# Head projection in rounded parts, and new orders around it, in a two-layer transformer kernel

## The chip, the cores and the metric

The kernel is one program on one core of a Trainium2 chip. The core has TensorE (PE in the profile) for matrix products and transposes into PSUM, VectorE (DVE), ScalarE (ACT) and GpSimd (POOL) for elementwise work, and SyncE (SP), which issues the DMAs. Each engine runs its own queue in order; semaphores tie them together. The metric is the device time of one execution in microseconds.

## The reference

The input x has 8 batches of 512 rows of 128 numbers. Each of two layers adds an attention part and a feed-forward part, both computed from the same normed rows.

Layer 0, attention: 16 heads of 64 (8 pairs), causal softmax, and an output projection of all heads. Layer 0, feed-forward: a shared expert and 32 experts of width 64, of which a router picks six per row with weights. Layer 1, attention: RMS norm, 4 query and 2 key heads of 32, normed queries and keys, output projection. Layer 1, feed-forward: three blocks of linear, layer norm, gelu, linear, with dequantized weights.

```
z   = einsum('dvh,bhcv->bcd', W, y) * (sqrt(d_embed / d_value) / num_heads)   # heads' projection
out = einsum('teh,te->th', y, combine) + shared_out                           # experts
x   = x + attention(xn) + ffn(xn)                                             # each layer
```

## The kernel before, in words

**Layer 0** goes batch by batch. A batch has eight attention rounds, one for each pair of heads, and then 17 units (the shared expert and 16 pairs of experts).

Most products of layer 0 are split products: each operand is kept as a rounded high part (type fp32r) and the rest as a low part, and `split_matmul` issues three products, high by high, high by low, low by high. ScalarE makes the high part with a copy. VectorE or GpSimd subtracts it to make the low part. The transposes, the products with the softmax rows and the heads' projection take plain float32 operands.

On TensorE, `slot` is one round: transposes of the last round's softmax rows (`turn_step`, steps 0, 1, 4, 3, 2), the projection of the next round's queries and keys (`project_qk`), the scores in three chunks (`score0`, `score_rest`) and the last round's values (`weigh_pair`). On ScalarE and VectorE `first_layer` is written in the same order.

`units` follows. For each unit u TensorE projects gate and up (`project_unit`), and three units later multiplies the hidden rows into ACC, a PSUM bank (`unit_down`). Between them ScalarE applies silu, VectorE multiplies by the up part (`gate`) and by the expert weights (`hidden`), ScalarE rounds (`high_part`), and the low part is subtracted by GpSimd for the units in `POOL_LO`, otherwise by VectorE (`low_part`). The rows of the next batch are transposed after unit 5, their router products come after unit 7 (`router_logits`), queries and keys after 9, values after units 12 to 15.

The outputs of the attention pairs, `yt`, are divided by the softmax sums on GpSimd (`divide_pair`), with the reciprocals spread over the partitions by a DMA into one of three `rrow` buffers. The tables `POOL_LO` and `SUMS_AFTER` give the unit after which each pair comes.

The heads' projection (`project_out(b, i)`, two pairs a call) adds `w_out0` times `yt` to ACC. Its four calls stand in `first_head`, at the beginning of the next batch: before and between the last three `unit_down`, and between the first score chunks. After the fourth ScalarE copies ACC.

**Layer 1** goes in two groups of four batches: the linear blocks and the projections of attention first, then eight attention rounds, then the output rows. Its order is written out by hand on each engine. On GpSimd `inv_sqrt`, `inv_norms` and `norm_qk` serve the norms, `add_rows1` adds the residual. The last linear step (`lin_out`, k = 2) adds the hidden rows by a product with the identity. The last batch's four projection calls stand around the first linear steps of layer 1. The last batch's output is one division, one set of products, one addition and one store.

## Time and profile before

| | us |
|---|---|
| median of 3 runs | 1227.32 (1227.23 to 1228.21) |
| the profiled execution | 1227.05 |
| its span in the trace | 1225.3 |
| instructions | 24028 |
| granted TensorE clock, mean | 1.0 of full speed |

The page gives for each engine how long it was busy. TensorE's matmul records overlap, since they are pipelined: a record's length is longer than the distance to the next start, and costs are best read from starts. LDWEIGHTS (PEld) run beside the products. A plain float32 product appears as two records, a rounded one as one. In a timeline row the first number is the start, the second the time from there to the end of the last of the merged instructions, "x4" the number merged.

### The profile page before, as it was taken

The numbers are of one execution on the slowest core, as the hardware profiler recorded it, in microseconds if no ns is written. First come the engines' busy times: TensorE is split into PE (matmuls) and PEld (weight loads), VectorE is DVE, ScalarE is ACT, GpSimd is POOL, SyncE is SP. The second block draws the span as 40 slices with busy tenths as digits, with TensorE's granted clock in tenths as the row PEclk, the third lists the DMA queues.
The fourth block names the chain that finished last, engine by engine and source line by source line (L and its number), as shares of the span: only waits on it lengthen the run. The fifth ranks groups of instructions, "written<-read, shape, count | busy, mean of one in ns | idle before, by whom it ended". The sixth has DMA issues, their size and how long they took to land.

```text
span 1225.3 us, 24028 instructions
## 1 busy us (share of the span) xinstructions
PE 1199.7 (98%) x8956; PEld 893.6 (73%) x8956; DVE 984.0 (80%) x1900; ACT 821.7 (67%) x2174; POOL 409.0 (33%) x362
## 2 busy tenths in 40 slices
PE   8999999999999999999999999999999999999997
PEld 6777677767776777677767786778677777767765
DVE  6878588968896889688968886889687877888786
ACT  6775577557756775677557755775577667777775
POOL 2216410640063007300630073007200859326910
PEclk9999999999999999999999999999999999999999
DMA  7004200410041014100410041004000500000000
GB/s 255 1 29 141 88 1 29 128 55 2 29 135 49 1 30 139 43 2 29 146 37 1 30 147 36 1 29 153 30 1 30 170 13 1 10 10 19 1 10 27
DMA packets 44275, 63.93 MB, mean 52 GB/s; under 512 B 8128, under 2 KB 18368, under 8 KB 43904
## 3 DMA queue, kind: packets, MB, share of 16 engines
q1 hardware_dynamic: 44160, 62.39, 16.1%
q8 instruction: 72, 1.18, 0.4%
q14 instruction: 43, 0.35, 0.1%
HBM read 59.48 MB, written 2.88 MB: 51 GB/s over the span
## 4 chain that ended last, share of the span: by engine, by line
PE 83%; DVE 7%; ACT 4%; POOL 2%; issue 1%; DMA 1%; SPq 1%; DVEq 0%; POOLq 0%
PE psum L1440 14%; PE psum L1396 14%; PE psum L1462 12%; PE psum L64 11%; PE psum L66 10%; PE psum L65 10%; PE psum L1499 4%; PE psum L1405 2%; ACT probs L734 2%; PE psum L1348 1%; DVE mneg L1098 1%; PE psum L1466 1%; DVE sg L1148 1%; DMA crow<-weights 1%; DVE stats L1207 1%
## 5 line engine op out<-in xcount | busy, mean ns | idle before, releaser
L734 ACT ACTIVATE probs<-psum,mneg 128x512 f32<-128x512 f32 (+3 forms) x640 | 329.9, 529 | 132.9 <-DVE mneg L1098 128.6
L1098 DVE TENSOR_REDUCE mneg<-psum 128x2 f32<-128x1024 f32 (+2 forms) x320 | 254.3, 820 | 118.4 <-PE psum L1405 118.2
L1440 PE MATMUL psum<-ident,probs 128*128 128x128 f32 x1600 | 224.8, 278 | 8.9 <-ACT pt L755 3.9
L1089 DVE COPY pt<-psum 128x512 f32<-128x512 f32 x320 | 205.9, 682 | 31.5 <-PE psum L1440 29.1
L1440 PEld LDWEIGHTS psum<-ident,probs 128*128 128x128 f32 x1600 | 176.4, 140 | 42.8 <-issue 24.4
L543 POOL TENSOR_TENSOR qk_lo<-sg,qk_hi 128x512 fp32r<-128x512 f32 x64 | 91.9, 1441 | 167.5 <-ACT qk_hi L778 167.5
L1462 PE MATMUL psum<-pt,v_all 128*64 128x384 f32 (+5 forms) x1088 | 142.6, 412 | 0.0
L507 POOL TENSOR_TENSOR rstd<-var,mhalf 128x4 f32<-128x4 f32 x7 | 7.1, 1011 | 404.5 <-DVE var L987 404.5
L734 ACT ACTIVATION_READ_ACCUMULATOR probs<-psum,mneg 128x1 f32 x640 | 132.3, 207 | 0.0
L1396 PE MATMUL psum<-qk_hi 64*128 64x512 f32 (+7 forms) x640 | 121.5, 375 | 1.3 <-ACT probs L734 1.1
L1462 PEld LDWEIGHTS psum<-pt,v_all 128*64 128x64 f32 (+1 forms) x1088 | 69.5, 135 | 66.2 <-issue 50.7
L64 PE MATMUL psum<-xt_hi,gu_hi 128*128 128x512 f32 x272 | 110.7, 407 | 0.0
L66 PE MATMUL psum<-xt_hi,gu_lo 128*128 128x512 f32 x272 | 107.7, 396 | 0.0
L65 PE MATMUL psum<-xt_lo,gu_hi 128*128 128x512 f32 x272 | 107.5, 395 | 0.0
L539 POOL TENSOR_TENSOR yt<-yt,rrow 128x512 f32<-128x512 f32 x64 | 99.7, 1563 | 23.0 <-DMA rrow<-sums 22.8
L1148 DVE TENSOR_TENSOR sg<-sg,crow 128x512 f32<-128x512 f32 x88 | 97.8, 1111 | 9.3 <-DMA crow<-weights 6.3
L1396 PE MATMUL psum<-qk_lo,qk_hi 64*128 64x512 f32 (+7 forms) x640 | 103.5, 319 | 0.0
L1396 PE MATMUL psum<-qk_hi,qk_lo 64*128 64x512 f32 (+7 forms) x640 | 103.4, 318 | 0.0
L788 ACT ACTIVATE sg<-psum 128x512 f32<-128x512 f32 x96 | 57.1, 595 | 56.3 <-PE psum L66 56.1
L1396 PEld LDWEIGHTS psum<-qk_hi 64*128 64x128 f32 (+1 forms) x640 | 60.1, 184 | 46.4 <-issue 44.3
L1138 DVE TENSOR_TENSOR sg<-sg,psum 128x512 f32<-128x512 f32 x96 | 65.3, 680 | 21.7 <-ACT sg L788 21.7
L778 ACT ACTIVATE qk_hi<-sg 128x512 fp32r<-128x512 f32 x96 | 60.3, 628 | 31.2 <-DVE sg L1148 31.2
(261 smaller groups left out, 2436.2 us busy)
## 6 DMA issues: line engine op xcount, KB each, us to landing
crow<-weights SPq DMA_DIRECT2D x256, 128.0 KB, 3.0
rrow<-sums SPq DMA_DIRECT2D x128, 128.0 KB, 3.0
gu_raw<-in_gu SPq DMA_DIRECT2D x1, 2176.0 KB, 11.4
x_all<-in_x SPq DMA_DIRECT2D x8, 256.0 KB, 6.4
out_rows<-x_all SPq DMA_DIRECT2D x8, 256.0 KB, 2.3
down_raw<-in_down SPq DMA_DIRECT2D x1, 1088.0 KB, 13.5
wqkv_raw<-in_wqkv SPq DMA_DIRECT2D x1, 896.0 KB, 6.7
wqkv_raw<-in_wqkv SPq DMA_DIRECT2D x1, 512.0 KB, 4.9
```

What stands on the lines that cost most here:

```text
L64: nc.tensor.matmul(out, lh, rh, start=start, stop=False, **kw)
L65: nc.tensor.matmul(out, lh, rl, start=False, stop=False, **kw)
L66: return nc.tensor.matmul(out, ll, rh, start=False, stop=stop, **kw)
L539: pool.tensor_tensor(yt[:, p, :], yt[:, p, :], rrow[:, n % RROWS, :], ALU.mult).then_inc(y_divided, 1)
L543: pool.tensor_tensor(hm_lo[u % 3], sg[u % 3], hm_hi[u % 3].bitcast(F32), ALU.subtract).then_inc(pool_lo_ready, 1)
L734: last = act.activation(probs[:, h * HALF + PROB[t]:h * HALF + PROB[t] + w], bank[score_bank(rnd, c) + h][:, o:o + w], ACT.Exp, bias=mneg[ ...
L1089: dve.tensor_copy(turned_rows(rnd)[:, s % 2, :, 3 - s // 2, :], bank[TURN_BANK[s]].rearrange("p (j q) -> p j q", q=P)).then_inc(pt_ready, 1)
L1098: last = dve.tensor_reduce(mneg_h[:, :, t], psum[:, b:b + 2, o:o + P * (t + 1)], AX, ALU.max, negate=True)
L1148: dve.tensor_tensor(sg[u % 3], sg[u % 3], crow[:, m % CROWS, :], ALU.mult).then_inc(hm_ready, 1)
L1396: mm(bank[score_bank(rnd, c) + h][:, o:o + w], ql[r, 0, qs_], kl[r, 1, ks], start=i == 0 and n == 0, stop=False, **K)
L1440: last = nc.tensor.transpose(bank[TURN_BANK[s]][:, i * P:(i + 1) * P], probs[:, v:v + P], ident[:, :])
L1462: last = mm(Y[c:c + m, first * P:T], v(k), rows_t[:, k, first:TILES, :].rearrange("p t q -> p (t q)"), start=(k == 0), stop=(k == TILES - ...
```

## The change

It has these parts.

- **Heads' projection in rounded parts.** The weights are split once in batch 0 (ScalarE rounds, GpSimd subtracts). For each batch ScalarE rounds the eight divided pairs (`high_values`, after the units in `Y_HIGH_AFTER`). GpSimd subtracts pairs 0 to 3 (after the divisions of pairs 4, 5 and 6), VectorE pairs 4 to 7 (after units 14 and 15 and behind the last unit). `project_out` issues split products.
- **Batch ends.** The third call of `project_out` moves behind the second score chunk. For the last batch all four calls stand behind its last `unit_down` and between the first transposes of layer 1.
- **Slots.** In rounds 2 to 6 the projection of the next queries moves from before the first score chunk to behind step 4, next to that of the keys. ScalarE takes the queries behind its copy of step 4. VectorE's router work stands before the second row maximum.
- **Router.** High and low weights lie side by side: the rows' high part is multiplied by all 64 columns at once, the low part by the 32 high ones. VectorE adds the two halves.
- **Layer 1.** The identity product of `lin_out` becomes a transpose that accumulates. GpSimd's `add_rows1` come earlier. The last batch's values, division, output rows, addition and store go in two halves of 256 rows. The table load after the last softmax is gone.
- **Space.** `stats`, `ss1`, `rn1`, the third `rrow` and `acc_cols` share room with other tensors.

```diff
+        Y_HIGH_AFTER = {8: [0], 11: [1, 2], 12: [3], 13: [4], 14: [5], 15: [6], 16: [7]}
+        POOL_Y_LO = {4: [0], 5: [1, 2], 6: [3]}
+        VECTOR_Y_LO = {14: [4], 15: [5], 16: [6, 7]}
+        LAST_POOL_Y_LO, LAST_VECTOR_Y_LO = [[0, 1], [4]], [[2, 3], [5, 6, 7]]
...
+            def low_values(b, pairs):                     # GpSimd; VectorE has the same with y_lo_ready
+                for p in pairs:
+                    pool.wait_ge(y_hi_ready, b * PAIRS + p + 1)
+                    pool.tensor_tensor(y_lo[:, p, :], yt[:, p, :], y_hi[:, PAIRS - 1 - p, :].bitcast(F32), ALU.subtract).then_inc(pool_y_lo_ready, 1)
             def units(b):
                 for u in POOL_LO:
                     low_part(b, u)
                     for p in POOL_LO[u]:
                         divide_pair(b, p)
+                        if b < B - 1:
+                            low_values(b, POOL_Y_LO.get(p, []))
...
-                inv_sqrt(0, 2)
-                add_rows1(1)
...
+                    for g in range(3):                    # first group; the second has them between inv_sqrt(0, g)
+                        add_rows1(g)
...
+            def high_values(b, pairs):
+                for p in pairs:
+                    act.wait_ge(y_divided, b * PAIRS + p + 1)
+                    act.activation(y_hi[:, PAIRS - 1 - p, :], yt[:, p, :], ACT.Copy).then_inc(y_hi_ready, 1)
...
+                    if b < B - 1 or u < UNITS - 2:
+                        high_values(b, Y_HIGH_AFTER.get(u, []))
...
-                chain.step(dve.tensor_reduce(sm, lg, AX, ALU.max, negate=True))
+                chain.step(dve.tensor_copy(rl[:, :, :], lg[:, :, 1, :]))
+                chain.step(dve.tensor_tensor(rl[:, :, :], rl[:, :, :], lg[:, :, 0, :], ALU.add))
+                chain.step(dve.tensor_reduce(sm, rl[:, :, :], AX, ALU.max, negate=True))
...
+                        if u < UNITS - 1:
+                            low_values(b, VECTOR_Y_LO.get(u, []))
                 low_part(b * UNITS + UNITS - 1, UNITS - 1)
+                if b < B - 1:
+                    low_values(b, VECTOR_Y_LO[UNITS - 1])
...
                 for p in (2 * i, 2 * i + 1):
-                    last = mm(ACC, w_out0[:, p, :], yt[:, p, :], start=False, stop=(p == PAIRS - 1), **K)
+                    last = split_matmul(nc, ACC, (w_out_hi[:, p, :], w_out_lo[:, p, :]), (y_hi[:, PAIRS - 1 - p, :], y_lo[:, p, :]), False, p == PAIRS - 1, **K)
...
-                    last = split_matmul(nc, logits_bank(b)[:, t * E:(t + 1) * E], (xt_hi[:, b % 2, c], xt_lo[:, b % 2, c]), (rw_hi[:, :], rw_lo[:, :]), True, True)
+                    mm(logits_bank(b)[:, o:o + 2 * E], xt_hi[:, b % 2, c], rw[:, :], start=True, stop=False, **K)
+                    last = mm(logits_bank(b)[:, o:o + E], xt_lo[:, b % 2, c], rw_hi, start=False, stop=True, **K)
...
-                if p < PAIRS - 1:
-                    pe.wait_ge(y_ready, n - 1) if p > 1 else pe.wait_ge(qk_lo_ready, n * 2 + 1)
+                if p == 1:
                     project_qk(n + 1, [0])
...
+                elif p < PAIRS - 1:
+                    pe.wait_ge(y_ready, n - 1)
+                    project_qk(n + 1, range(2))
...
                 first_chunks(b)
+                score0(b * PAIRS, 1)
                 if b:
                     project_out(b - 1, 2)
-                score0(b * PAIRS, 1)
...
-            project_out(B - 1, 0)
             unit_down(B - 1, UNITS - 3)
...
+            unit_down(B - 1, UNITS - 1)
+            project_out(B - 1, 0)
             lin_in(0, 0, 2)
...
-                        mm(bank[g][:, c], ht[g][:, c], ident[:, :], start=False, stop=False, **K)
+                        mm(bank[g][:, c], ht[g][:, c], ident[:, :], is_transpose=True, start=False, stop=False, **K)
...
+                def last_rows(g):
+                    for half in range(2):
+                        pe.wait_ge(y_divided, ROUNDS0 + n0 + g + 1 + half)
+                        for t in range(2 * half, 2 * half + 2):
+                            c = slice(t * P, (t + 1) * P)
+                            last = mm(last_banks(half)[1][:, c], y1t[g][:, c], wo1[:, :], start=True, stop=True)
+                        last.then_inc(rows_done, 1)
```

## Rows read from the trace of the kernel before

**Rows 1.** The page, busy time of each engine and its share of the span.
```profile
PE 1199.7 (98%) x8956; PEld 893.6 (73%) x8956; DVE 984.0 (80%) x1900; ACT 821.7 (67%) x2174; POOL 409.0 (33%) x362
```
**Rows 2.** The page, chain that ended last, by engine.
```profile
PE 83%; DVE 7%; ACT 4%; POOL 2%; issue 1%; DMA 1%; SPq 1%; DVEq 0%; POOLq 0%
```
**Rows 3.** Busy time by stretch: stretch, us, each engine busy (instructions), clock, DMA.
```profile
213.00:261.00 48.00, 48.00 (x224) 37.06 (x222) 42.09 (x60) 28.56 (x51) 33.01 (x25) 1.00 0.41 122
```
**Rows 4.** Timeline of TensorE where batch 1 ends: start, us, engine, line, operation.
```profile
257.41 1.88 PE L1499 MATMUL psum<-yt,w_out 128*128 128x512 f32 x4
...
259.36 0.40 PE L65 MATMUL psum<-hm_third,down_hi 128*128 128x512 f32 x1
...
259.82 1.88 PE L1499 MATMUL psum<-yt,w_out 128*128 128x512 f32 x4
...
262.23 0.39 PE L64 MATMUL psum<-qk_hi,down_hi 128*128 128x512 f32 x1
...
263.98 1.98 PE L1499 MATMUL psum<-yt,w_out 128*128 128x512 f32 x4
265.90 0.44 PE L1396 MATMUL psum<-qk_hi 64*128 64x384 f32 x2
...
269.24 1.98 PE L1499 MATMUL psum<-yt,w_out 128*128 128x512 f32 x4
271.06 1.04 PE L1440 MATMUL psum<-ident,probs 128*128 128x128 f32 x8
```
**Rows 5.** Timeline of TensorE: first router product, and what follows the twelfth.
```profile
229.27 0.18 PE L64 MATMUL psum<-rw_hi,xt_hi 128*128 128x32 f32 x1
...
230.53 0.48 PE L64 MATMUL psum<-qk_hi,down_hi 128*128 128x512 f32 x1
```
**Rows 6.** The page, a group of ScalarE: busy, mean ns, idle before.
```profile
L778 ACT ACTIVATE qk_hi<-sg 128x512 fp32r<-128x512 f32 x96 | 60.3, 628 | 31.2 <-DVE sg L1148 31.2
```
**Rows 7.** Timeline of VectorE, last units of batch 1.
```profile
244.12 1.79 DVE L1142 TENSOR_TENSOR qk_lo<-sg,qk_hi 128x512 fp32r<-128x512 f32 x1
...
251.63 1.36 DVE L1148 TENSOR_TENSOR probs<-probs,crow 128x512 f32<-128x512 f32 x1
...
255.39 1.78 DVE L1142 TENSOR_TENSOR hm_third<-probs,hm_third 128x512 fp32r<-128x512 f32 x1
...
258.87 1.47 DVE L1142 TENSOR_TENSOR qk_lo<-sg,qk_hi 128x512 fp32r<-128x512 f32 x2
```
**Rows 8.** Timeline of GpSimd, the same stretch.
```profile
251.14 1.29 POOL L543 TENSOR_TENSOR qk_lo<-sg,qk_hi 128x512 fp32r<-128x512 f32 x1 [2.18 <-ACT qk_hi L778]
252.47 1.67 POOL L539 TENSOR_TENSOR yt<-yt,rrow 128x512 f32<-128x512 f32 x1
255.17 1.45 POOL L539 TENSOR_TENSOR yt<-yt,rrow 128x512 f32<-128x512 f32 x1 [1.03 <-DMA rrow<-sums]
```
**Rows 9.** Timeline of TensorE at the end of layer 0.
```profile
981.39 1.88 PE L1499 MATMUL psum<-yt,w_out 128*128 128x512 f32 x4
...
983.80 0.39 PE L1670 MATMUL psum<-bias_bf,bias_on 96*128 96x512 bf16 x1
```
**Rows 10.** Timeline of TensorE in layer 1, identity and linear product of a tile.
```profile
1036.31 0.39 PE L1737 MATMUL psum<-ident,room 128*128 128x128 f32 x2
1036.53 0.39 PE L1738 MATMUL psum<-lin,room 128*128 128x128 f32 x2
```
**Rows 11.** Timeline of TensorE in a slot, four transposes and their follower.
```profile
204.68 0.60 PE L1505 MATMUL psum<-ident,rrow 128*128 128x128 f32 x4
205.12 1.04 PE L1440 MATMUL psum<-ident,probs 128*128 128x128 f32 x8
```
**Rows 12.** The chain that ended last, its end: start, us, what.
```profile
1219.84 0.70 DVE yt L1332
...
1220.68 1.14 PE psum L1796 x8
...
1221.85 0.69 DVE x_all L1288
```

More of the change, by code:

```diff
@@ L150, in build @@
         sg_third = probs[:, 3 * T:4 * T]
-        rrow = sb("rrow", [P, RROWS, T])
+        rrow = sb("rrow", [P, 2, T])
+        rrow0 = [rrow[:, 0, :], rrow[:, 1, :], probs[:, 4 * T:5 * T]]
+        with ExitStack() as units:
+            y_hi = units.enter_context(nc.sbuf_tensor("y_hi", [P, PAIRS, T], F32R))
         pt = sb("pt", [P, 2, TILES, TILES, P])
+        with ExitStack() as units:
+            y_lo = units.enter_context(nc.sbuf_tensor("y_lo", [P, PAIRS, T], F32R))
         yt = sb("yt", [P, PAIRS, T])
@@ L177, in build @@
         nmr = sb("nmr", [P, TT])
-        ss1 = sb("ss1", [P, G, TILES * (H1 + KV1)])
-        rn1 = sb("rn1", [P, G, TILES * (H1 + KV1)])
+        ss1, rn1 = (v[:, :, :].rearrange("p t e -> p (t e)")[:, 0:G * TILES * (H1 + KV1)].rearrange("p (g n) -> p g n", g=G) for v in (corr, left))
         with ExitStack() as first:
@@ L248, in rows1_bank, with last_banks @@
             return bank[3] if g == G - 1 else bank[7]
+        def last_banks(half):
+            return (bank[0], bank[2]) if half else (bank[6], bank[3])
         def copied1(n):
@@ L489, in _ @@
                     sp.wait_ge(lin_ready, 1)
-            for b in range(B):
+            for b in range(B - 1):
                 sp.wait_ge(rows_ready, b + 1)
                 sp.dma_start(out_v[b, :, :, :], x_all[:, b, :, :]).then_inc(stored, 16)
-            sp.wait_ge(stored, 16 * B)
+            for half in range(2):
+                t = slice(half * TILES // 2, (half + 1) * TILES // 2)
+                sp.wait_ge(rows_ready, B + half)
+                sp.dma_start(out_v[B - 1, :, t, :], x_all[:, B - 1, t, :]).then_inc(stored, 16)
+            sp.wait_ge(stored, 16 * (B + 1))
         @block.gpsimd
@@ L1148, in hidden, with low_values @@
                 dve.tensor_tensor(sg[u % 3], sg[u % 3], crow[:, m % CROWS, :], ALU.mult).then_inc(hm_ready, 1)
+            def low_values(b, pairs):
+                for p in pairs:
+                    dve.wait_ge(y_hi_ready, b * PAIRS + p + 1)
+                    dve.tensor_tensor(y_lo[:, p, :], yt[:, p, :], y_hi[:, PAIRS - 1 - p, :].bitcast(F32), ALU.subtract).then_inc(y_lo_ready, 1)
             def add_rows(b):
@@ L1325, in _ @@
                 add_attention(G - 2)
+                if q + 1 == GROUPS:
+                    dve.wait_ge(rrow_ready, n0 + G)
+                    halves = [slice(h * T // 2, (h + 1) * T // 2) for h in range(2)]
+                    for h, c in enumerate(halves):
+                        dve.wait_ge(y_done, ROUNDS0 + n0 + G + h)
+                        dve.tensor_tensor(y1t[G - 1][:, c], last_banks(h)[0][:, c], rrow[:, 0, c], ALU.mult).then_inc(y_divided, 1)
+                    x, past = (v.rearrange("p t d -> p (t d)") for v in (x_all[:, B - 1, :, :], xn1[G - 1]))
+                    for h, c in enumerate(halves):
+                        dve.wait_ge(rows_done, n0 + G + h)
+                        dve.tensor_tensor(x[:, c], last_banks(h)[1][:, c], past[:, c], ALU.add).then_inc(rows_ready, 1)
+                    break
                 if q + 1 < GROUPS:
@@ L1702, in weigh_batch, with weigh_last @@
                                  [((pt, pt1)[j][:, h, :, :, :], lambda k, c=v1 + j * HD1: qkv1[g][:, k, c:c + HD1]) for j in range(2) for h in range(2)], HD1)
+                def weigh_last(g):
+                    v1 = (H1 + KV1) * HD1
+                    rnd = ROUNDS0 + (n0 + g) * 2 + 1
+                    pe.wait_ge(pt4_ready, rnd + 1)
+                    pe.wait_ge(pt_ready, (rnd + 1) * (TURNS - 1))
+                    heads = [((pt, pt1)[j][:, h, :, :, :], v1 + j * HD1) for j in range(2) for h in range(2)]
+                    for half in range(2):
+                        Y = last_banks(half)[0]
+                        for k in range(2 * half + 2):
+                            lo, hi = max(k, 1, 2 * half), 2 * half + 2
+                            for i, (rows_t, c) in enumerate(heads):
+                                last = mm(Y[i * HD1:(i + 1) * HD1, lo * P:hi * P], qkv1[g][:, k, c:c + HD1], rows_t[:, k, lo:hi, :].rearrange("p t q -> p (t q)"),
+                                          start=(k == 0), stop=(k == 2 * half + 1), tile_position=(0, i * HD1), **K)
+                        if half == 0:
+                            for i, (rows_t, c) in enumerate(heads):
+                                last = mm(Y[i * HD1:(i + 1) * HD1, 0:P], qkv1[g][:, 0, c:c + HD1], rows_t[:, 3, 2, :], start=False, stop=True,
+                                          tile_position=(0, i * HD1), **K)
+                        last.then_inc(y_done, 1)
                 def project_qkv(g):
@@ L1797, in output_rows @@
                     last.then_inc(rows_done, 1)
+                def last_rows(g):
+                    for half in range(2):
+                        pe.wait_ge(y_divided, ROUNDS0 + n0 + g + 1 + half)
[3 more added lines that the diff above has]
+                        last.then_inc(rows_done, 1)
                 def head_rows1(r):
```

107 lines of the change are left out of this document (70 added, 37 removed).

## The prediction

> **What bounds the kernel now.** I read the page's busy times first: TensorE is busy 98% of the span [rows 1]. Its idle time adds up to 25.6 us (1225.3 - 1199.7), so a gain has to come out of what TensorE executes. The chain of waits says the same, PE 83% [rows 2]. Then I read the busy time by stretch over the expert stage of one batch: PE 48.00 of 48.00 us, VectorE 42.09, GpSimd 33.01, ScalarE 28.56 [rows 3]. So one microsecond less matmul there is one microsecond less time, as long as the low halves of the split operands come in time. VectorE, with 6 us left, and GpSimd, with 15, are the ones that can be late. Last I read the timeline of TensorE, VectorE and GpSimd where one batch ends and the next begins.
>
> **Heads' projection, what TensorE saves.** All starts are from one boundary [rows 4]. A rounded 512-column product goes every 0.23 us (259.36 to 259.82 holds two), so a split product of three is 0.70. The first plain call (two pairs of heads, four records) and one down product take 257.41 to 259.82 = 2.41, so the call is 1.71. It becomes six rounded products, 1.40: 0.31 saved, and the second call has the same cost. The third is 263.98 to 265.90 = 1.92. It moves behind the second score chunk, next to rounded products, so both changes of kind go: 1.40 is left, 0.52 saved. The fourth is 269.24 to 271.06 = 1.82 and becomes 1.50 (0.1 for starting after a bf16 mask): 0.31 saved. Sum 1.45 per batch, seven boundaries: 10.2 us.
>
> **Router.** Twelve 32-column products take 229.27 to 230.53, 0.105 each [rows 5]. Eight are left, four of them 64 wide. The trace has no 64-wide one with 128 rows. Its bounds are the 0.105 of the narrow and the 0.23 of the 512-wide; I take 0.11, nearest to the narrow. That leaves 0.88: 0.4 saved, eight times, 2.8 in the seven expert stages and 0.4 at the start. VectorE gets a copy and an addition of 128 elements, some 0.6 us, beside a stage where it has slack [rows 3]; nothing.
>
> **What the projection adds elsewhere.** Per batch ScalarE gets eight roundings of 0.63 [rows 6], 5 us. It is busy 28.56 of 48 [rows 3]: hidden. Batch 0 also splits the weights once, ScalarE and GpSimd, in slots: 0 to 1 us, taken as 0 against the slot order below. GpSimd gets four subtractions, VectorE four. Here is the doubt. Subtractions and products with both inputs in SBUF (the code's `low_part` and `hidden`) show two lengths on VectorE. At 251.63 one lasts 1.36, and it ends 0.56 after GpSimd's operation that began at 251.14 and ended at 252.43. At 255.39 one lasts 1.78 and ends 0.55 after GpSimd's of 255.17 to 256.62. GpSimd's of 252.47 ends at 254.14, 1.15 after VectorE's at 252.99 [rows 7, 8]. So the two engines take turns, 0.55 and 1.15 us. The one that comes second waits for all of the other's instruction.
>
> The Trainium skill (SBUF — State Buffer, section "Who interferes with whom") states just that: a VectorE instruction with two SBUF inputs and a GpSimd one that reads SBUF exclude each other, and the second to issue blocks until the first finishes. The rows agree, and the rule speaks against this change: by it the eight new subtractions cost more than their lengths. Without it they would be 4 x 0.6 on VectorE, hidden.
>
> Slack first. TensorE used low part 15 and 16 at 262.23 and just before. VectorE had finished the pair at 258.87 + 1.47 = 260.34, so 1.9 us in hand [rows 4, 7]. TensorE also arrives 1.0 us sooner (0.4 router, 0.62 from two calls), so VectorE may be late by at most 0.9 before TensorE stands.
>
> Lower end of the delay: if new subtractions fall into gaps of GpSimd, VectorE's own two before that point (pairs 4 and 5, 1.1 us) fit its gaps, and the stall is 0. Upper end: a walk in which GpSimd always has its next operation ready. VectorE's subtraction of 244.12 ended at 245.91 [rows 7]. From there GpSimd has nine operations to the end of its last division, four of them new, 9 x 1.15, with seven VectorE turns of 0.55 between: 260.1. Behind that VectorE still has the pair 5 subtraction, the last gate, product, low part 15, ScalarE's rounding, low part 16, six steps of about 0.6: 263.7. Low part 14, between the eighth and ninth, comes at 259.1, where TensorE wants it at 258.0: 1.1 stall. The last pair then comes at 263.0 and 263.7 for a TensorE that has used that time for two more calls: 1.8 more. Together 2.9 us per boundary, 2.0 for the first batch, which has no statistics of the batch before on either engine.
>
> Which? The rows show turns that VectorE had to wait for beside turns that were free (two subtractions free in 1.47 at 258.87, against 1.36 to 1.79 for one that waits [rows 7]). GpSimd also had a gap of over 2 us before 251.14 that the walk closes completely. I take 1.2 us per boundary, a little under the middle: 8.4 for seven. Behind the waiting VectorE stands the row maximum of the next batch's first scores, which waits for TensorE anyway.
>
> **Slots and batch ends.** In slots 2 to 6 the query projection moves behind the first score chunk and step 4. Transposes to scores cost what transposes to projection to scores did, so TensorE's sum is unchanged; 0, with 1 us to either side for ScalarE's order in batch 0. The router work moved ahead of a row maximum shifts 1 us of VectorE within a slot: 0.
>
> **Last boundary.** All four projection calls go behind the last unit. TensorE did the first from 981.39 and came to the bias product at 983.80 [rows 9]. That waits for the last gate, so now TensorE arrives after one down product and stands 1.2. Four calls save 1.3, and pair 5 to 7's low parts sit between VectorE statistics that the norms wait for. Bounds -1.3 and +1.5; I take +0.5.
>
> **Second layer.** The identity product of the last linear step is two passes, together 0.22 per tile (1036.31 to 1036.53) [rows 10]; as a transpose it is 0.11 (four in 0.44, 204.68 to 205.12) [rows 11]. Four tiles, eight calls: 3.5 us of TensorE. Half of the calls stand beside norms that other engines deliver later anyway, so 1.8. On GpSimd two additions of 512 elements leave the run before the norms (an undelayed operation of that size takes 1.29 [rows 8]); behind them VectorE's statistics are the next late thing, so 1.0 of 2.5 in the first group, nothing in the second. The dropped table load was hidden behind the last transposes: 0.
>
> **Tail.** Division 0.70, output products 1.14, addition 0.69 in series after the last value products [rows 12]. In halves the first half's division and products run under the second's: 0.4, 0.57, 0.4 are left with one more semaphore hop, 1.1 saved; between 0.3 (if the second store's issue waits behind the first's) and 1.3.
>
> **The sum.** Profiled execution 1227.05 (span 1225.3 and 1.75 around it; the median of the runs is 1227.32). TensorE -10.2 - 2.8 - 0.4 = -13.4; port turns +8.4; last boundary +0.5; second layer -2.8; tail -1.1. Together -8.4: 1218.6, and 1219 against the median.
>
> **The rivals.**
> 1. The low parts are wholly hidden: -16.8, 1210. For it: GpSimd idles 15 of 48 us [rows 3], and pairs 0 to 3 are wanted late. Against: the lengths in [rows 7, 8], each already stretched.
> 2. The turns eat everything, slower than before. Mechanism: VectorE and GpSimd exclude each other from the eleventh unit on, low parts 14 to 16 are late, and TensorE stands before the down products at each boundary. At 2.9 a boundary the turns cost 19.4, net +2.6: 1230. With a turn of 1.84 us instead of 1.70 (GpSimd's undelayed 1.29 and VectorE's 0.55) the walk ends 1 us later, 24.5 in all, +7.7: 1235. It decides from about 2.4 us of stall per boundary. For it: the turns are seen at every meeting in [rows 7, 8]. Against: those rows have gaps, which it leaves out. By the rule of the Trainium skill named above (SBUF — State Buffer, "Who interferes with whom") this is the way that it goes; the trace agrees with the blocking and doesn't show whether gaps are left.
> 3. The gain isn't there: the rounded calls save less than 0.3 because a change of kind costs the rounded ones too, and the stall is as forecast. At a third of the 10.2 (3.4) the sum is -1.6, 1226. Against: rounded products follow each other at 0.23 throughout [rows 4].
>
> **How the numbers follow.** Forecast 0.42, rival 1 0.24, rival 2 0.22, rival 3 0.12. A difference of 0.2%, about 2.5 us, is what a measurement can tell here. Faster: forecast and rival 1, 0.66 less the forecast's upper edge, 0.64. Slower 0.21, the same 0.15. Range 1208 to 1232: from a little below rival 1 to between rival 2's two prices.
>
> **What would show it.** Right: the projection's records are three to a pair with starts 0.23 apart; the down products after the first two calls wait 1 to 1.5 us in all for VectorE; the period from one boundary's first call to the next one's falls by about 0.7. Rival 1: it falls by 1.85 and TensorE waits for nothing. Rival 2: GpSimd is busy without a gap from unit 11 on, and a wait of 2.5 us or more stands before the down products. The forecast is also wrong if the last boundary, where the change puts four calls among norms, grows by more than 1.5 us.

## The result, and the profile after

The changed kernel is slower than the kernel before, by 0.4%.

| | before | changed |
|---|---|---|
| median of 15 runs, us | 1227.53 (1227.06 to 1233.58) | 1233.18 (1229.54 to 1237.76) |
| ratio of changed to before | | 1.0040, 95% interval 1.0029 to 1.0051 |
| profiled execution, us | 1227.05 | 1236.99 |
| its span, us | 1225.3 | 1235.2 |

1219 was forecast, with a range from 1208 to 1232. The median is above the range. A time is 1.8 us longer than the span of the same execution. The page of the changed kernel, busy times and chain of waits:

```profile
PE 1191.8 (96%) x8972; PEld 907.0 (73%) x8972; DVE 1041.4 (84%) x1951; ACT 856.1 (69%) x2237; POOL 466.5 (38%) x394
```
```profile
PE 58%; DVE 24%; issue 6%; ACT 5%; DMA 3%; SPq 2%; POOL 1%; DVEq 0%; ACTq 0%
```

Against [rows 1, 2] TensorE is busy 7.9 us less, and its idle time grew from 25.6 to 43.4 us. In the chain its share fell from 83 to 58%, and VectorE's rose from 7 to 24%. The waits of TensorE (who it waited for, us in total, times, longest) name the places:

```profile
PE psum L64 <- DVE qk_lo L1209: 7.3, 8, 1.6
PE psum L64 <- DVE rl L1094: 6.3, 5, 1.6
...
PE psum L64 <- DVE hm_third L1209: 2.9, 3, 1.2
PE psum L1438 <- ACT yt L954: 2.4, 2, 1.2
```

The first and third stand before the down products, the second before the next batch's projection of queries and keys (it waits for the router's numbers), the fourth before a norm's transposes in layer 1.

Where the 9.9 us between the two spans are, worked out from the starts of the first gate/up product of each batch (332.41 in the trace before and 337.99 after for batch 2, for instance) and of the first `project_qkv` product of each group:

| stage | changed less before, us |
|---|---|
| start and batch 0's slots | +5.6 |
| batch 0's units to batch 1's units | -0.4 |
| the six periods that follow | +3.8 (0.33, 0.60, 0.57, 0.65, 1.46, 0.20) |
| last units and last boundary | +3.1 |
| layer 1, first group | +0.7 |
| layer 1, second group, and tail | -3.0 |

**One steady batch.** The stretch of [rows 3] in batch 2, the kernel before first, then the changed one:

```profile
334.50:382.50 48.00, 48.00 (x224) 36.96 (x222) 41.16 (x60) 28.22 (x50) 31.01 (x25) 1.00 0.38 121
```
```profile
340.00:388.00 48.00, 46.75 (x222) 36.99 (x221) 43.44 (x60) 30.43 (x56) 35.07 (x24) 1.00 0.40 122
```

TensorE's timeline of the changed kernel there, the wait at unit 9 and the end of the batch:

```profile
362.86 0.47 PE L64 MATMUL psum<-xt_hi,wqkv_hi 128*128 128x512 f32 x1 [1.25 <-DVE rl L1094]
...
385.30 0.40 PE L64 MATMUL psum<-y_hi,w_out_hi 128*128 128x512 f32 x1
...
386.69 0.39 PE L64 MATMUL psum<-hm_third,down_hi 128*128 128x512 f32 x1
...
388.53 0.39 PE L66 MATMUL psum<-y_hi,w_out_lo 128*128 128x512 f32 x1
390.14 0.50 PE L64 MATMUL psum<-qk_hi,down_hi 128*128 128x512 f32 x1 [1.23 <-DVE qk_lo L1209]
```

The call of two pairs takes 385.30 to 386.69, 1.39, against 1.71 in [rows 4]: TensorE's saving is what was forecast. The waits eat it. VectorE and GpSimd in the same stretch:

```profile
359.86 0.69 DVE L1215 TENSOR_TENSOR sg<-sg,crow 128x512 f32<-128x512 f32 x1 [1.77 <-DMA crow<-weights]
360.47 0.28 DVE L1091 COPY rl<-psum 128x128 f32<-128x128 f32 x1
...
361.44 1.28 DVE L1094 TENSOR_TENSOR rl<-rl,route_sum 128x128 f32<-128x128 f32 x1
...
381.26 1.78 DVE L1220 TENSOR_TENSOR y_lo<-yt,y_hi 128x512 fp32r<-128x512 f32 x1
...
386.38 1.78 DVE L1220 TENSOR_TENSOR y_lo<-yt,y_hi 128x512 fp32r<-128x512 f32 x1
...
389.40 1.47 DVE L1209 TENSOR_TENSOR qk_lo<-sg,qk_hi 128x512 fp32r<-128x512 f32 x2
```
```profile
367.82 1.29 POOL L577 TENSOR_TENSOR qk_lo<-sg,qk_hi 128x512 fp32r<-128x512 f32 x1 [2.25 <-ACT qk_hi L830]
...
377.34 3.45 POOL L582 TENSOR_TENSOR y_lo<-yt,y_hi 128x512 fp32r<-128x512 f32 x2
380.75 1.75 POOL L577 TENSOR_TENSOR qk_lo<-sg,qk_hi 128x512 fp32r<-128x512 f32 x1
382.45 1.75 POOL L573 TENSOR_TENSOR yt<-yt,rrow 128x512 f32<-128x512 f32 x1
384.16 1.75 POOL L582 TENSOR_TENSOR y_lo<-yt,y_hi 128x512 fp32r<-128x512 f32 x1
385.86 1.75 POOL L573 TENSOR_TENSOR yt<-yt,probs 128x512 f32<-128x512 f32 x1
```

From 371.77 on GpSimd runs without a gap, most of its operations 1.75 us long where one that waits for nothing lasts 1.29 [rows 8] (earlier in the batch gaps are left, 2.25 us before 367.82), and VectorE's subtractions among them last 1.78 instead of 0.68. From the wait at 359.86 to the last low part VectorE has no gap above 0.1 us. That low part (the end of `qk_lo` L1209) comes 52.9 us after the batch's first gate/up product; in the trace before it came at 49.6. The router's last addition reads only SBUF now (before, one input was in PSUM), and it lasts 1.28 instead of the 0.29 of the operations ahead of it.

**Layer 1.** A wait, and the stretches behind it (the column before the last two is the granted clock):

```profile
1043.92 0.66 PE L1438 MATMUL psum<-ident,yt 128*128 128x128 f32 x4 [1.21 <-ACT yt L954]
```
```profile
1044.00:1046.00 2.00, 2.00 (x16) 1.37 (x18) 0.33 (x1) 1.90 (x3) 2.00 (x3) 0.88 0.00 0
1046.00:1048.00 2.00, 2.00 (x17) 1.57 (x16) 1.11 (x2) 1.96 (x5) 2.00 (x2) 0.50 0.00 0
1048.00:1050.00 2.00, 2.00 (x10) 1.92 (x9) 1.08 (x2) 1.27 (x5) 1.84 (x3) 0.50 0.00 0
...
```

Before, this wait was 0.30 and the clock stayed at 1.00 throughout. Here it was 0.50 for 6.8 us, which is 1.2 of 2.4 GHz. In the start it fell too, from 8 to 18 us.

### The profile page after: what moved, and what is told of

Same layout as the page of the kernel before. It is cut to its first block, busy times and chain, and to the rows that moved or that the text cites. A ratio compares the mean times of both kernels' runs of the same rounds, so it can differ in the third digit from the quotient of the medians.

```text
span 1235.2 us, 24206 instructions
## 1 busy us (share of the span) xinstructions
PE 1191.8 (96%) x8972; PEld 907.0 (73%) x8972; DVE 1041.4 (84%) x1951; ACT 856.1 (69%) x2237; POOL 466.5 (38%) x394
## 4 chain that ended last, share of the span: by engine, by line
PE 58%; DVE 24%; issue 6%; ACT 5%; DMA 3%; SPq 2%; POOL 1%; DVEq 0%; ACTq 0%
PE psum L1530 13%; PE psum L1486 13%; PE psum L1552 11%; PE psum L64 5%; PE psum L65 4%; PE psum L66 4%; DVE sg L1215 4%; DVE sg L1205 3%; DMA crow<-weights 3%; ACT probs L786 2%; DVE mneg L1165 2%; DVE probs L1215 2%; PE psum L1495 2%; DVE qk_lo L1209 2%; DVE probs L1205 2%
## 5 line engine op out<-in xcount | busy, mean ns | idle before, releaser
L1215 DVE TENSOR_TENSOR sg<-sg,crow 128x512 f32<-128x512 f32 x88 | 100.7, 1144 | 10.4 <-DMA crow<-weights 7.5
L1145 DVE SCALAR_TENSOR_TENSOR qk_lo<-psum,qk_hi 128x512 fp32r<-128x512 f32 x72 | 49.0, 681 | 39.0 <-ACT qk_hi L799 38.9
```

The source lines that it names most:

```text
L1215: dve.tensor_tensor(sg[u % 3], sg[u % 3], crow[:, m % CROWS, :], ALU.mult).then_inc(hm_ready, 1)
```

## Experiments

Each edit is to the changed kernel unless it says otherwise; code is shortened. Times are medians; the ratio is to the kernel before, run on the same chip (medians 1227.87 to 1228.37), with its 95% interval. "Mean clock" is the granted clock over a whole run. Differences of stages are between single executions and can hold an accident of either: the last units and boundary of experiment 15, which edits nothing there, are 0.7 us shorter than before.

**1. The projection waits only for the router's bank.**

```
-    chain.step(dve.tensor_tensor(rl, rl, lg[:, :, 0, :], ALU.add))
+    dve.tensor_tensor(rl, rl, lg[:, :, 0, :], ALU.add).then_inc(logits_taken, 1)
+    dve.wait_ge(logits_taken, b + 1)
-    pe.wait_ge(rl_ready, b + 2)        # before project_qk, unit 9
+    pe.wait_ge(logits_taken, b + 2)
```

> The changed kernel, but TensorE's next heads' projection waits only until VectorE has read the router's bank (its second operation), not for all four operations. In the changed kernel TensorE stood 1.15 to 1.6 us for VectorE's last router operation in five of seven batches, and 1.25 us more before the down products. Theory A (VectorE is the bound from the ninth unit to the boundary: it had 0.2 to 1.9 us idle there against 2.4 to 4.7 before, and its last low part came 3.0 us later): the first wait goes and the second grows by the same; the time stays within 1 us of the changed kernel, about 1232, ratio to the kernel before 1.003 to 1.004. Theory B (the router's wait is a cost of its own): 5 x 1.15 us are saved, about 1227, ratio 0.999 to 1.000.

Measured: 1233.18, ratio 1.0035 (1.0024 to 1.0047). The time is theory A's, but the second wait did not grow: the first moved on to the next things that VectorE makes, as TensorE's timeline of batch 2 shows:

```profile
364.88 0.50 PE L64 MATMUL psum<-xt_hi,gu_hi 128*128 128x512 f32 x1 [0.58 <-DVE sg L1206]
...
383.07 0.51 PE L64 MATMUL psum<-hm_third,down_hi 128*128 128x512 f32 x1 [0.45 <-DVE hm_third L1210]
...
386.69 0.51 PE L64 MATMUL psum<-qk_hi,down_hi 128*128 128x512 f32 x1 [1.26 <-DVE qk_lo L1210]
```

0.58 + 0.45 + 1.26 = 2.29 instead of 1.25 + 1.23 = 2.48.

**2. No subtractions for the projection in batches 0 to 6.** The products read `y_hi` in place of `y_lo`, so the low parts are missing from the output.

```
-    low_values(b, POOL_Y_LO.get(p, []))        # GpSimd, units of batches 0 to 6
-    low_values(b, VECTOR_Y_LO.get(u, []))      # VectorE
```

> The changed kernel without the eight subtractions for the heads' projection in batches 0 to 6 (four on GpSimd, four on VectorE); TensorE does the same three products per pair and reads the rounded part in the place of the low part, so its output is not the reference's. Theory A (VectorE, lengthened by its own four subtractions and by turns with GpSimd, is the bound): VectorE gets back 2.4 us of its own and the turns, all stalls of TensorE in the expert stage and at the boundary go (1.15 + 1.25 each), 7 x 2.4 = 16 us less, about 1217. Theory B (the router's wait is a cost of its own, only the boundary's stall comes from the subtractions): 7 x 1.25 = 9 us less, about 1224.

Measured: 1219.24, ratio 0.9924 (0.9911 to 0.9936), 14 us less. That is nearer to A. The boundary's waits are gone, the router's stayed (6.1 us in five waits), so part of B holds: without the subtractions VectorE is no longer the bound and the router's wait counts. In the two periods without that wait the period is 1.65 and 1.96 less than before, about the prediction's saving of 1.85 on TensorE; in the four with it, 0.51 to 1.17 less.

**3. The router as before.** Twelve products, two operations on VectorE.

```
+    chain.step(dve.tensor_reduce(sm, lg, AX, ALU.max, negate=True))
-    (copy of one half, addition of the other, maximum, addition in SBUF)
+    dve.tensor_tensor(rl, lg, over_experts(sm), ALU.add)
```

> The changed kernel with the router as before: twelve 32-wide products, and on VectorE two operations instead of four, the last with an input in PSUM. Theory A (VectorE is the bound): it gets back 0.64 us of operations and, where the last addition fell on a GpSimd operation (1.28 instead of 0.29 in the trace), 1.0 more: 0.6 to 1.6 a batch, 4 to 11 us in all, although TensorE has 0.4 more to do: 1222 to 1228. Theory C (the router's change is good for TensorE and VectorE has room, as the prediction had it): 3 us more, about 1235.

Measured: 1231.77, ratio 1.0029 (1.0019 to 1.0040): 1.4 less, within the intervals of the changed kernel, neither A nor C. The router's wait is gone, but all six steady periods are 0.65 to 0.86 longer than before (0.20 to 1.46 in the changed kernel). Giving VectorE back 0.6 to 1.6 us bought next to nothing, so its own work is hardly the bound. "VectorE is the bound" had to be made narrower: the turns that it takes with GpSimd are (theory D, which experiments 5 and 6 try).

**4. Before, with layer 1's part alone.** The kernel before with the change's edits in `lin_out`, `add_rows1` (order), `weigh_last`, `last_rows`, the last additions and stores, and without the last table load:

```
-    mm(bank[g][:, c], ht[g][:, c], ident, start=False, ...)
+    mm(bank[g][:, c], ht[g][:, c], ident, is_transpose=True, start=False, ...)
-    add_rows1(1)                    # and 2 and 0 later
+    for g in range(3):              # first group, behind inv_sqrt(0, 2)
+        add_rows1(g)
```

> The kernel before with only the second layer's part of the change: identity products as transposes, the additions on GpSimd in the new order, no last table load, and the tail in halves. The prediction gave these 2.8 and 1.1 us: 1223.6, ratio 0.9968. The changed kernel's trace shows 1.5 us less in the second group of batches, 1.5 in the tail and 0.5 to 1.4 in the first group, 1223 to 1224. Rival: the first group's part was only the recovery of the time lost just ahead of it; then 3.0 less, 1224.5.

Measured: 1226.23, ratio 0.9986 (0.9978 to 0.9995), 1.6 less, not 3 to 4. The trace has -2.4 in the first group and -1.3 in the second with the tail. The second would be 1.6 more at full clock: the traces without a low clock there have -2.9, and this one has 0.50 for 3.4 us from 1151.1. The last units and boundary are 1.1 longer, with a wait that TensorE did not have before:

```profile
998.41 0.66 PE L1369 MATMUL psum<-ident,yt 128*128 128x128 f32 x4 [1.52 <-DVE yt L1228]
```

It is for VectorE's normalised rows. These, in the kernel before, in this one and in the changed one:

```profile
994.78 1.12 DVE L1219 TENSOR_SCALAR yt<-x_all,mv,rstd 128x128 f32<-128x128 f32 x4 [3.00 <-PE psum L1499]
```
```profile
995.72 2.63 DVE L1228 TENSOR_SCALAR yt<-x_all,mv,rstd 128x128 f32<-128x128 f32 x4 [2.99 <-PE psum L1520]
```
```profile
1004.06 4.03 DVE L1295 TENSOR_SCALAR yt<-x_all,mv,rstd 128x128 f32<-128x128 f32 x4
```

The additions that were moved earlier now run on GpSimd beside them. In the changed kernel TensorE waits only 0.30 for the 4.03, since it stands 0.79 and 1.08 for other things just before; what the additions cost there is not separated.

**5 and 6. Without GpSimd's four subtractions; without VectorE's four.** In batches 0 to 6; of the two lines that experiment 2 takes out, 5 takes the first and 6 the second.

> The changed kernel without GpSimd's four subtractions (pairs 0 to 3) in batches 0 to 6; VectorE keeps its four; TensorE reads the rounded part in the place of the missing low one, so its output is not the reference's. Theory D (turns: GpSimd's operations and VectorE's with two SBUF inputs exclude each other, and together they fill the stretch from the ninth unit to the boundary, 17 x 1.25 + 13 x 0.57 = 29 of 30 us): 4 x 1.25 us of turns go, all of TensorE's boundary stall (1.25, really some 2 us a batch with what its overlapping ends hide) goes, 9 to 14 us less, 1219 to 1224. Theory E (VectorE has too many operations of its own): VectorE still has them, its operations only wait less, 2 us less at most, 1231.

> The changed kernel without VectorE's four subtractions (pairs 4 to 7) in batches 0 to 6, GpSimd keeps its four; its output is not the reference's. Two of the four stood ahead of the last low parts, 1.78 and 0.68 to 1.78 us each. Theory D (turns): 2 x 0.6 to 2 x 1.2 us less ahead of the last low part, 1.2 to 2 us a batch, 8 to 12 less, 1221 to 1225. Theory E: the same or more. The pair of this kernel and the one without GpSimd's subtractions tells: by D GpSimd's are worth as much as VectorE's or more, by E next to nothing.

Measured: 1221.48, ratio 0.9942 (0.9929 to 0.9955), and 1222.75, ratio 0.9956 (0.9944 to 0.9969). Either engine's four are worth 10 to 12 us, both not much more (14), so D holds and E falls: with all its own subtractions left, and in their old places, VectorE is in time when GpSimd's are gone. TensorE waits before no down product of batches 0 to 6 in either trace. The low parts of the hidden rows on VectorE (busy, mean ns), which both kernels have alike, in the changed kernel and in 5:

```profile
L1209 DVE TENSOR_TENSOR qk_lo<-sg,qk_hi 128x512 fp32r<-128x512 f32 x32 | 35.0, 1096 | 0.7
```
```profile
L1207 DVE TENSOR_TENSOR qk_lo<-sg,qk_hi 128x512 fp32r<-128x512 f32 x32 | 26.2, 822 | 0.7
```

**7. VectorE's subtractions behind the last low part.** One line, nothing left out:

```
-        VECTOR_Y_LO = {14: [4], 15: [5], 16: [6, 7]}
+        VECTOR_Y_LO = {16: [4, 5, 6, 7]}
```

> The changed kernel with all four of VectorE's subtractions behind its last low part (pairs 4 and 5 were ahead of it), nothing left out. Theory D: the last low parts come 1.3 to 2.5 us sooner, TensorE's stall of 1.25 before the down products goes in all seven batches, 5 to 9 us less, 1224 to 1228. Rival: four subtractions in one go stand ahead of the row maxima of the next batch's first scores, the stall comes back behind those scores (0.6 x 2 = 1.2 us a batch) and the time stays at 1232 to 1233.

Measured: 1223.03, ratio 0.9951 (0.9937 to 0.9964), 10 us less, faster than both. The group of these subtractions on VectorE (busy, mean ns), changed kernel first, then this one, and this one's timeline at the end of batch 2:

```profile
L1220 DVE TENSOR_TENSOR y_lo<-yt,y_hi 128x512 fp32r<-128x512 f32 x33 | 34.9, 1081 | 0.0
```
```profile
L1220 DVE TENSOR_TENSOR y_lo<-yt,y_hi 128x512 fp32r<-128x512 f32 x33 | 20.6, 682 | 0.0
```
```profile
384.77 1.47 DVE L1209 TENSOR_TENSOR qk_lo<-sg,qk_hi 128x512 fp32r<-128x512 f32 x2
386.16 2.49 DVE L1220 TENSOR_TENSOR y_lo<-yt,y_hi 128x512 fp32r<-128x512 f32 x4
388.57 2.41 DVE L1165 TENSOR_REDUCE mneg<-psum 128x2 f32<-128x1024 f32 x3
```

Where GpSimd has finished, four subtractions take 2.49 us; among its operations two took 2 x 1.78 and held up the last gate and product as well. No wait is left before the down products of batches 0 to 6, and the row maxima that stand behind the four cost nothing visible. This run alone does not tell turns from VectorE's own order: two subtractions of 0.6 us less ahead of the last low part are 8.4 us in seven batches by themselves. Experiment 5, which leaves that order as it is, tells.

**8. The last batch's first call back ahead of a down product.**

```
+    project_out(B - 1, 0)
     unit_down(B - 1, UNITS - 3)
     ...
     unit_down(B - 1, UNITS - 1)
-    project_out(B - 1, 0)
```

> The changed kernel with the last batch's first projection call (pairs 0 and 1) back ahead of the down product of unit 14, GpSimd making the two low parts within the units. In the changed kernel's trace TensorE stood 0.96 and 1.56 us before the last down products of this batch, and the last boundary was 3.7 us longer than before. Theory F (the calls are missing as filler for these waits): 1.4 us of work moves into the waits, 1.4 less, 1231.7 at the level of the changed kernel. Rival: the waits are set by VectorE's last low parts, which GpSimd's two extra turns in the units make later by up to 1.1: within 0.5 us of the changed kernel.

Measured: 1230.79, ratio 1.0024 (1.0016 to 1.0033), 2.4 less, but the trace does not support the theory: last units and boundary are 4.3 us above before, against 3.1 in the changed kernel, with a wait of 1.88 for GpSimd. Inconclusive, since the interval overlaps that of the changed kernel.

**9 to 12. A mended kernel and three variants of it.** To experiment 7 it adds experiment 1's wait, the last batch's calls in their old order with six low parts on GpSimd, one of the additions in an earlier gap, and the rounding of the weights in slot 7.

```
-    if b == 0 and p == len(GU_PIECES):   act.activation(w_out_hi, w_out0, ACT.Copy)
+    if b == 0 and p == PAIRS - 1:        act.activation(w_out_hi, w_out0, ACT.Copy)
+    project_out(B - 1, 0); unit_down(14); lin_in(0); unit_down(15); lin_in(1)
+    project_out(B - 1, 1); lin_in(2); unit_down(16); project_out(B - 1, 2)
```

> The changed kernel with the late subtractions of the kernel before this one (1223.0) and three more edits, each in a stage of its own: the projection waits only for the router's bank; the last batch's calls in their old order (pairs 0 and 1 ahead of unit 14's down product, 2 and 3 behind the first linear step, and so on), GpSimd making six of the eight low parts; the rounding of the output weights in slot 7 instead of slot 4. Expected: 0.5 to 1.1 us less in the four or five batches with the router's wait (VectorE has 2 us idle there now); 2 to 4 us less at the last boundary (stalls of 1.78 + 0.32 + 0.78 + 1.09 us, and the low granted clock behind them); 1.3 us less in the slots. About 1216, ratio 0.990. Rival: VectorE and GpSimd stay the bound and the waits only move, 1221.

```
-    WARM, WARM_BETWEEN = 9, 3
+    WARM, WARM_BETWEEN = 11, 4
```

> The mended kernel with more idle-time products ahead of the first transposes (11 instead of 9, and 4 instead of 3 behind them). In the changed kernel's trace TensorE stood 1.20 us there and 0.54 later, and the granted clock fell to 0.50 from 8 to 18 us: 4 us lost. If a wait brings the fall, it is rarer here: 1 to 2 us less than the mended kernel in the median and less spread, clock 0.999 to 1.000. Rival: the fall does not hang on these waits: same clock and time, or up to 0.4 us more.

```
-    mm(bank[g][:, c], ht[g][:, c], ident, is_transpose=True, ...)
+    mm(bank[g][:, c], ht[g][:, c], ident, is_transpose=g > 1, ...)
```

> The mended kernel with the identity product of the second layer's last linear step in two passes again for the first two batches of each group, transposes for the other two. Theory: those first transposes only lengthen TensorE's wait for the next norm (1.21 us instead of 0.30), behind which the granted clock fell in several traces: the time stays the same or falls by up to 1.5 us. Rival (the prediction's price for them): 0.9 us more in each group whose wait does not cover them, up to 1.8 more.

```
-    add_rows1(0); ...; add_rows1(1); add_rows1(2)       # first group
+    add_rows1(1); ...; inv_sqrt(1, 2); add_rows1(2); add_rows1(0)
```

> The mended kernel with GpSimd's additions of the first group in the order of the kernel before (one behind the third norm, two behind the fourth step). The prediction gave the new order 1.0 us: then this is 1.0 more. Theory G: the new order takes away a wait of 1.6 us in the second step, but its additions fall beside VectorE's normalised rows (1.12 us before, 2.63 and 4.03 us with the new order) and cost 1.5 us there: within 0.5 us of the mended kernel.

| | median | ratio, interval | runs at a mean clock of 0.997 or less |
|---|---|---|---|
| 9 mended | 1221.83 | 0.9943 (0.9931 to 0.9955) | 5 of 5 |
| 10 fuller start | 1220.93 | 0.9941 (0.9929 to 0.9953) | 5 of 5 |
| 11 two passes for two batches | 1218.26 | 0.9919 (0.9906 to 0.9931) | 0 of 4 |
| 12 additions in the old order | 1221.86 | 0.9956 (0.9944 to 0.9968) | 5 of 6 |

9 is only 1.2 below experiment 7, not the 7 expected. Each of its three edits mostly moved a cost. The router's wait of 1.14 became one of 0.6 to 0.8 some 6 us later. The weights' rounding costs 0.9 in slot 7 (8.39 us for 7.45) and 0.3 are left in slot 4, instead of 1.4 there. Last units and boundary stayed 3.8 us above before: low parts moved into the units made GpSimd late there (a wait of 2.14). 12 is undecided: its median is that of 9, its ratio 0.0013 (1.6 us) higher, and the intervals overlap. In the two traces, each with one stretch of low clock in the first group, the old order is 1.6 us longer in that group and 0.4 shorter at the last boundary. That is nearer to the prediction's 1.0 for the new order than to theory G. 11 is the surprise: with *more* work on TensorE it is 3.6 faster. The same place in 9 and then in 11, each by TensorE's timeline (the wait) and the stretches around it (the clock):

```profile
1029.21 0.66 PE L1436 MATMUL psum<-ident,yt 128*128 128x128 f32 x4 [1.21 <-ACT yt L951]
```
```profile
1026.00:1030.00 4.00, 2.79 (x24) 2.31 (x23) 2.79 (x5) 3.15 (x9) 3.84 (x6) 1.00 0.00 0
1030.00:1034.00 4.00, 4.00 (x33) 3.03 (x32) 2.52 (x3) 3.71 (x8) 4.00 (x3) 0.69 0.00 0
```
```profile
1028.05 0.66 PE L1436 MATMUL psum<-ident,yt 128*128 128x128 f32 x4 [0.29 <-ACT yt L951]
```
```profile
1026.00:1030.00 4.00, 3.71 (x34) 2.84 (x35) 1.95 (x5) 3.41 (x7) 3.84 (x7) 1.00 0.00 0
1030.00:1034.00 4.00, 4.00 (x42) 3.66 (x38) 3.01 (x4) 3.96 (x13) 3.84 (x4) 1.00 0.01 2
```

**13 and 14. Plain calls for the last batch, and a fuller start.** 13 is 11 with these edits; GpSimd joins the weights in a slot of the last batch.

```
+    pool.tensor_tensor(w_plain, w_out_hi.bitcast(F32), w_out_lo.bitcast(F32), ALU.add)
     def project_out(b, i):          # b == B - 1
+        last = mm(ACC, w_plain[:, p, :], yt[:, p, :], start=False, ...)
```

> The kernel with two-pass products for the first two batches (1218.3), with the last batch's four calls as plain float32 again: GpSimd adds the two parts of the output weights once, in its idle time in the last batch's slots, and no head of this batch is rounded. Theory D (turns): in the changed kernel the last batch has to pay for eight roundings and eight subtractions where VectorE and GpSimd have no room; units and last boundary took 3.1 to 4.9 us more than before in every trace with rounded calls there. Without them they take what they took before: 3 to 4 us less, about 1214.5 to 1215.5. Rival: the last boundary is longer for the moved additions and the transposes, not for the rounded calls: within 1 us of 1218.3.

> The same kernel with the longer idle-time products at the start (11 and 4 instead of 9 and 3). If the low granted clock at the start depends on TensorE's waits there: the highest of its times lies nearer to the lowest, median 0.3 to 1 us less. Rival: no difference, or 0.4 more.

Measured: 13 1213.97, ratio 0.9891 (0.9876 to 0.9906); 14 1213.76, ratio 0.9886 (0.9871 to 0.9901). The ratio is 0.0028 below that of 11, 3.4 us. Last units and boundary are 0.6 and 0.9 *below* before (as in experiment 15, no more than an accident), against 3.8 above in 11: the rounded calls had cost the last batch about 4 us, more than they save there. 13 and 14 are the same, so the fuller start shows nothing. This is the fastest version; its page:

```profile
PE 1188.9 (98%) x8980; PEld 905.6 (75%) x8980; DVE 1023.4 (84%) x1946; ACT 852.6 (70%) x2229; POOL 460.0 (38%) x392
```
```profile
PE 67%; DVE 17%; ACT 7%; issue 4%; DMA 2%; POOL 2%; SPq 1%; DVEq 0%; ACTq 0%; POOLq 0%
```

**15. Before, with the transposes of the first two batches alone.** One word added to one line (`is_transpose=g < 2`).

> The kernel before with one edit: the identity product of the last linear step as a transpose in the first two batches of each group (TensorE executes 8 x 0.11 = 0.9 us less per group, ahead of the wait for the fourth norm, 0.30 us before). Theory H: the work saved turns into wait (0.30 to 1.2 us), and behind it the granted clock falls in a part of the executions, 1.5 us or more each time: slower than before by 0.5 to 2.5 us, 1228 to 1230. Rival (the prediction's price, half of the calls hidden, no clock): the same time as before, 1227.5.

Measured: 1228.83, ratio 1.0010 (1.0001 to 1.0020), against 1227.89. 4 of its 11 runs had a mean clock of 0.997 or less, none of the 21 runs of the kernel before did. Those four have spans of 1229.5 in the mean, the other seven 1226.3, the kernel before 1226.1. That is the time of theory H: less work, no gain in the good case and 3.2 us lost in the other.

**16. The changed kernel with two passes there.**

> The changed kernel with one edit: two passes again for the identity product of the first two batches of each group. Theory H: the wait of 1.21 us ahead of the fourth norm is 0.3 again, the fall of the granted clock behind it (3.1 us in the changed kernel's trace at 1045 to 1053) does not come: 1.5 to 3 us less, 1230 to 1231.7. Rival: the same 1233 or up to 1.8 us more.

Measured: 1229.95, ratio 1.0016 (1.0008 to 1.0025), 3.2 less, just beyond what H gave. Experiments 11, 15 and 16 show that these transposes bring the low clock (runs at 0.997 or less: 5 of 5 against 0 of 4, 4 of 11 against 0 of 21, 11 of 15 against 1 of 11). They don't show that the wait does: each edit changes both the wait (0.30 or 1.21) and what TensorE does ahead of it (products with the identity, or transposes), and no run has one without the other.

## Why the prediction was wrong

**Projection on TensorE (-10.2 for seven) and router (-0.4 each): right.** The first call takes 1.39 for 1.40, the third 1.50 for 1.40 (in the changed trace it follows a bf16 mask, 393.81 to 395.31), the router 0.81 for 0.88, and the period without waits is 1.65 to 2.10 below before (experiments 2 and 5), for 1.85 forecast.

**Port turns (+1.2 a boundary): the failed step.** The prediction saw the mechanism and priced it at half: it took 1.2 because GpSimd had gaps in the old trace, and they closed. The six steady periods are 0.6 longer in the mean, where the forecast had them 0.65 shorter, so with the 1.85 saved the loss is 2.5. The subtractions make 1.9 of it (without them, in experiment 2, the six periods are 1.2 shorter than before in the mean); most of the rest is the router's wait. The walk had 2.9 as its upper end and described what happened: from its start on GpSimd without a gap, VectorE waiting for whole operations. Rival 2 is the outcome; it had 0.22, and its prices were 1230 and 1235. The four runs at a mean clock of 0.999 or 1.000 took 1229.5 to 1232.6. That the number fits is in part luck: the last boundary, a slot and the clock, which rival 2 left as forecast or did not have, are in it too. Its mark was a wait of 2.5 before the down products. It shows as 1.25 there and 1.15 to 1.6 at unit 9, two places for one shortage (experiment 1). By the rule of the Trainium skill (SBUF — State Buffer, section "Who interferes with whom"), a VectorE operation with two SBUF inputs and a GpSimd one that reads SBUF exclude each other for the whole instruction. The trace agrees (1.78 for 0.68, 1.75 for 1.29), and so do experiments 5 and 6. The forecast should have gone by the blocking that its own rows showed, and not by the gaps in a trace that did not yet hold the new operations.

**VectorE's router operations, "some 0.6 us ... nothing": wrong in kind, small in effect.** The last addition lost its PSUM input and with it entered the turns (1.28). The wait that it makes, 1.14 to 1.57, costs some 0.7 a period where the subtractions are gone (experiment 2: 1.1 gained in most periods with it, 1.8 in those without); with them it is worth nothing (experiments 1 and 3).

**Slots and batch ends (0 to 1 us for the weights' rounding, taken as 0): +1.4.** ScalarE's second pass over the weights stands before a copy that TensorE waits for; slot 4 lasts 10.48 instead of 9.07:

```profile
67.82 1.06 ACT L886 ACTIVATE w_out_hi<-w_out 128x1024 fp32r<-128x1024 f32 x1
69.51 0.63 PE L1530 MATMUL psum<-ident,probs 128*128 128x128 f32 x4 [1.21 <-ACT pt L807]
```

**Last boundary (+0.5, bounds -1.3 and +1.5): outside its bounds.** +3.1 with the last units, 3.1 to 5.4 in every trace with rounded calls there, -0.6 with plain calls. The prediction named this as a sign of being wrong (growth by more than 1.5). The step counted waits of 1.2 and the calls' saving, not that the last batch's eight low parts have no slack to go to: the last units are as tight as the others, and behind them come norms.

**Layer 1 (-1.8 and -1.0) and tail (-1.1).** At full clock the first group is 2.4 and the second 1.5 shorter, 3.9 for 2.8. Half of the transposes give nothing, as the prediction had it: with two passes in their place (experiment 16) the groups are as short, 2.4 and 1.5. But it held them for free, and they cost the clock. The tail gave 1.5 for 1.1.

**The granted clock: not in the prediction.** 11 of the changed kernel's 15 runs have a mean clock of 0.997 or less and spans of 1232.3 in the mean; the other four have 1229.4. Experiments 15 and 16 show the transposes' part, about 3 us in the runs that it hits. It is not the whole: six of the thirteen traces of kernels with rounded calls in the last batch have the clock at 0.50 for 3.4 us between 976 and 996 us, around its last units, and none of the five traces with plain calls there has. The fall at the start in the profiled execution (4 us) is not explained: experiments 10 and 14 didn't show that a fuller start prevents it.

By size, from 1219 to 1233: turns and the router's wait 8.0 (7.7 in the six steady periods, 0.3 in the first), last boundary 2.6, slot 1.4, clock about 3 in the median run, less 1.5 that layer 1 and the tail gave beyond the forecast. Together 13.5 of 14.2, from one trace and so good to about 1 us.

## What to carry to other kernels

Where two engines exclude each other, sum the work of both over the stretch, at the lengths that they have when they wait, and compare it with the stretch; the slack of each alone says nothing, and a gap in the old trace is where the new operation goes. Put operations that are wanted late behind the last one that is wanted soon: one line of order was worth 10 us of 1233 here. Shortening TensorE's work ahead of a wait that other engines end gained nothing here, and the shortened form cost the clock in a part of the runs: after such an edit look at the granted clock of every run, not at the busy time.

## What was not expected of the hardware

- VectorE's normalised rows have one tensor input in SBUF and two per-partition scalars, and still lasted 2.63 and 4.03 us instead of 1.12 beside GpSimd's additions, four operations merged. In experiment 13, where they ran between the additions (at 986.95, the additions at 985.53 and 988.39), they lasted 1.11. So operations with one tensor input were held up too; how was not tried by itself.
- Of 13 traces of kernels with the transposes in the first two batches (a wait of 1.20 or 1.21 us ahead of the fourth norm in each group), 10 show a fall of the granted clock behind one of the two waits or both; of the five with a wait of 0.29 or 0.30 there none does. Whether the wait or the transposes bring it, and what else decides when it falls, stays open.
